# Two cross attentions: the score product from split rows placed by transfers, in the 32-bit rounded type, instead of a full 32-bit product over masked keys

## The reference, cut to what matters

```python
qh, kh, vh = (proj(q, Wq, bq), proj(k, Wk, bk), proj(v, Wv, bv))      # (b, 16, 512 or 77, 8)
scores = einsum('bhqd,bhkd->bhqk', qh, kh) / sqrt(8)
attn = softmax(scores, axis=-1)     # block 3: with a mask, and one more column of zero score in the sum
x = x + proj_out(einsum('bhqk,bhkd->bhqd', attn, vh))
```

## Time and profile before

| | |
|---|---|
| median of 3 runs | 1113.5 us (1104.1 to 1117.23) |
| the profiled execution, its own time | 1112.59 us |
| its span, first to last instruction | 1110.7 us |
| mean granted clock of TensorE | 0.871 |
| busy: PE, VectorE, ScalarE, POOL | 886.1, 599.1, 399.6, 225.2 us |
| l1x, 297 to 462 us | 165 us |
| l3x, 616 to 757 us | 141 us |

### The profile page before, as it was taken

The page is one execution under the profiler, slowest core; times in us unless marked ns, Lnnn a source line. Parts: engine busy times, 40 slices in busy tenths (PEclk is TensorE's granted clock), DMA queues, the critical chain, the costliest instruction groups (busy, mean ns, idle before and its releaser), DMA issues.

```text
span 1110.7 us, 15554 instructions
## 1 busy us (share of the span) xinstructions
PE 886.1 (80%) x5734; PEld 497.6 (45%) x5734; DVE 599.1 (54%) x1614; ACT 399.6 (36%) x687; POOL 225.2 (20%) x228
## 2 busy tenths in 40 slices
PE   5788985986776777569589799976888889886987
PEld 2334553653432343347457434333334334332887
DVE  4455554433535544435473355548687887773553
ACT  2344322332231322111042143331676565555423
POOL 1100051225142122124431000021000100004254
PEclk7799786999985876669889899996999998997999
DMA  9900001132043500031200200021212121103443
GB/s 282 303 25 1 1 31 45 55 94 69 24 128 83 167 25 23 29 90 37 64 2 4 76 1 1 1 61 54 80 54 79 39 74 42 39 20 122 153 156 114
DMA packets 56369, 76.35 MB, mean 69 GB/s; under 512 B 8318, under 2 KB 35070, under 8 KB 55608
## 3 DMA queue, kind: packets, MB, share of 16 engines
q1 hardware_dynamic: 50984, 66.08, 19.1%
q0 software_dynamic: 5312, 9.29, 2.6%
HBM read 46.76 MB, written 31.65 MB: 71 GB/s over the span
## 4 chain that ended last, share of the span: by engine, by line
PE 55%; DVE 20%; issue 10%; ACT 4%; DMA 3%; POOL 3%; another core or an unknown queue 3%; SPq 2%; POOLq 0%; DVEq 0%; ACTq 0%
PE PS L183 48%; DVE KB L1998 5%; PE PS L666 2%; DVE KB L1600 2%; DVE Ht L1514 1%; DVE st L1501 1%; POOL RB L2297 1%; SPq L2359 1%; DVE ON L1667 1%; POOL dbuf L2217 1%; DVE OT L1642 1%; POOL ve L2190 1%; PE PS L674 1%; DVE CX L1642 1%
## 5 line engine op out<-in xcount | busy, mean ns | idle before, releaser
L1998 DVE TENSOR_REDUCE KB<-PS 128x2 fp32r<-128x1024 f32 x128 | 154.4, 1220 | 36.6 <-PE PS L183 35.1
L1277 ACT ACTIVATE PT<-PS 77x512 f32<-77x512 f32 x192 | 98.1, 590 | 178.5 <-PE PS L183 178.5
L183 PE MATMUL PS<-CX 32*77 32x512 f32 (+2 forms) x896 | 129.3, 589 | 22.5 <-DVE OT L1642 10.5
L2190 POOL TENSOR_TENSOR ve<-ve,nh 128x4 f32<-128x4 f32 x40 | 41.3, 1032 | 441.4 <-DVE ve L1509 441.2
L1600 DVE TENSOR_REDUCE KB<-PS 128x16 fp32r<-128x1232 f32 x48 | 69.1, 1439 | 73.8 <-PE PS L183 73.8
L1433 ACT ACTIVATE PT<-PS 128x1024 f32<-128x1024 f32 x74 | 75.6, 1023 | 54.9 <-PE PS L183 52.7
L183 PE MATMUL PS<-QB,KB 64*128 64x512 f32 x256 | 61.9, 480 | 31.1 <-DVE KB L1998 19.7
L183 PEld LDWEIGHTS PS<-CX 32*128 32x128 f32 (+1 forms) x896 | 50.2, 199 | 67.2 <-issue 19.2
L183 PE MATMUL PS<-KB,QB 64*128 64x512 f32 x256 | 66.9, 523 | 6.0 <-DVE KB L1998 4.7
L183 PE MATMUL PS<-PT,VB 77*32 77x512 f32 x384 | 57.3, 672 | 6.7 <-DVE KB L1600 5.0
L183 PE MATMUL PS<-PT,RB 128*32 128x256 f32 x592 | 59.5, 410 | 1.5 <-ACT PT L1433 1.4
(11 more groups left out here) (330 smaller groups left out, 1548.6 us busy)
## 6 DMA issues: line engine op xcount, KB each, us to landing
S<-RA SPq DMA_DIRECT2D x20, 256.0 KB
QB<-zq SPq DMA_DIRECT2D x16, 256.0 KB, 2.7
KB<-zk SPq DMA_DIRECT2D x64, 64.0 KB, 2.4
dbuf<-in_c_fill SPq DMA_DIRECT2D x1, 2580.0 KB, 21.6
RB<-d SPq DMA_DIRECT2D x10, 256.0 KB
o<-CX SPq DMA_DIRECT2D x10, 256.0 KB, 2.3
CX<-RA SPq DMA_DIRECT2D x10, 256.0 KB
RA<-in_l_w SPq DMA_DIRECT2D x1, 2304.0 KB, 11.1
```

Source lines behind the costliest of these rows:

```text
L183: return e.matmul(o, l, r, start=first, stop=last, skip_group_check=True)
L1277: e.activation(slot[s][0:NK, :], PS[0:NK, 4 + j, :], ACT.Exp, bias=0.0, scale=a.scale).then_inc(*expd(i, r, j))
L1998: e.tensor_reduce(o, PS[:, k:k + 2, :], AX, ALU.max).then_inc(*rmax("s", s, t, p2))
L2190: e.tensor_tensor(ve[:, 8 * par + 4:8 * par + 8], ve[:, 8 * par:8 * par + 4], nh[:, :], ALU.pow).then_inc(*rstd(*key))
```

## The change

For l1x and l3x, the score product of `cross_back` alone is replaced. Queries and keys are each split into a rounded part (hi) and a remainder (lo), and laid out so that the 24 rows of one head are (hi, lo, hi) for queries and (hi, hi, lo) for keys; their product is hi*hi + lo*hi + hi*lo. Per unit, POOL makes the two parts (`CAST STG<-CX`, `TENSOR_TENSOR STG<-CX,STG`, each 128x512), SP writes them by three transfers to the DRAM tensor `zq1`, and reads them back by four into `QP1` (`RR<-zq`), a tile of type fp32r at RA's address. Once for l1x and once for l3x the same is done with the keys (128x312). The maximum is still computed from `a.km` and still subtracted by the selector product. As QP1 and KP1 lie over RA, they can be written only after the last expert product of block 0, and the loads of block 3's expert weights move from hook "l1x0" to `first(s)`, 16 pieces of 256 KB in the self attention.

```diff
+        QP1 = [RR[:, 2048 * n:2048 * n + 2048] for n in range(2)]
+        KP1 = RR[:, 6912:8192]
+        QHL = [STG[:, 0:512], STG[:, 512:1024]]
+        KHL = [KN[:, 0:CK], KN[:, 512:512 + CK]]
...
                 for r in range(4):
+                    if not a.expo:
+                        w.wait_ge(*kr1.at("k", a.n0, 3))
+                        w.wait_ge(*ld["l1"].all())
+                        w.wait_ge(*qr1[i % 2].at(i, 3))
                     for j in range(4):
                         w.wait_ge(*banks.take_at(4 + j, expd, i, r, j))
-                        mm(e, PS[0:NK, 4 + j, :], a.km[32 * j:32 * j + 32, b, r, :], Q[32 * j:32 * j + 32, r * a.nq // 4, :], True, False)
+                        if a.expo:
+                            mm(e, PS[0:NK, 4 + j, :], a.km[32 * j:32 * j + 32, b, r, :], Q[32 * j:32 * j + 32, r * a.nq // 4, :], True, False)
+                        else:
+                            mm(e, PS[0:NK, 4 + j, :], KP1[32 * j:32 * j + 24, CK * r + NKP * b:CK * r + NKP * b + NK],
+                               QP1[i % 2][32 * j:32 * j + 24, 512 * r:512 * r + 512], True, False)
...
+            def ahead(i):                                   # gpsimd
...
+                w.wait_ge(*qact.at(i, 0))
+                w.wait_ge(*(qw1[(i - 1) % 2].at(i - 1 if i != 20 else 11, 2) if i > 8 else (None, 0)))
+                e.tensor_copy(QHL[0], Q).then_inc(*split("qhi", i))
+                w.wait_ge(*split.at("qhi", i))
+                e.tensor_tensor(QHL[1], Q, QHL[0].bitcast(F32), ALU.subtract).then_inc(*split("qlo", i))
...
+            def queries(i):                                 # sync
+                w.wait_ge(*qw1[i % 2].at(i, 2))
+                w.wait_ge(*(scored.at(before[i], 3, 3) if before[i] >= 8 else e0.at("d", 2 * NT0 - 1)))
+                w.wait_ge(*down0.at(7))
+                for j in range(4):
+                    e.dma_start(QP1[i % 2][32 * j:32 * j + 24, :].rearrange("p (r c) -> p r c", r=4).bitcast(F32),
+                                zq1[i % 2][4 * j:4 * j + 4, :, :].rearrange("r p c -> p r c")).then_inc(*qr1[i % 2](i, j))
+
+            def ahead(i):                                   # sync
...
+                w.wait_ge(*split.at("qhi", i))
+                e.dma_start(z[:, 0:8, :], QHL[0].bitcast(F32)).then_inc(*qw1[i % 2](i, 0))
+                e.dma_start(z[:, 16:24, :], QHL[0].bitcast(F32)).then_inc(*qw1[i % 2](i, 1))
+                w.wait_ge(*split.at("qlo", i))
+                e.dma_start(z[:, 8:16, :], QHL[1].bitcast(F32)).then_inc(*qw1[i % 2](i, 2))
...
+                w.wait_ge(*scored.at(23, 3, 3))             # sync, first(s)
+                if s < 8:
+                    load("l3f", w1g[:, s, :], A["l3_w1"][s])
+                else:
+                    load("l3f", w2g[:, s - 8, :, :], A["l3_w2"][s - 8].rearrange("(c p) n -> p c n", p=128))
...
                     load("l1f", w2e, A["l1_w2"].rearrange("e (c p) n -> p e c n", p=128))
-                    for b in range(NB):
-                        w.wait_ge(*down0.at(4 + b))
-                    load("l3f", w1g, A["l3_w1"].rearrange("e p n -> p e n"))
-                    load("l3f", w2g, A["l3_w2"].rearrange("e (c p) n -> p e c n", p=128))
```

More of the change, by code:

```diff
@@ L241, in program @@
         zqk = [[nc.dram_tensor(f"z{n}{b}", (512, 512), F32, kind="Internal").ap() for b in range(NB)] for n in "qk"]
+        zq1 = [nc.dram_tensor(f"zq1{n}", (16, 24, 512), F32, kind="Internal").ap() for n in range(2)]
+        zk1 = [nc.dram_tensor(f"zk1{n}", (16, 25, CK), F32, kind="Internal").ap() for n in range(2)]
         x1 = nc.dram_tensor("x1", (NB * S, 128), F32, kind="Internal").ap()
@@ L429, in program @@
         d0e, comb = signal("d0e"), signal("comb")
+        split = signal("split")
         pinit, rstd, xrow = signal("pinit"), signal("rstd"), signal("xrow")
@@ L1173, in prepare @@
                         w.wait_ge(*kcD.at(a.n0 - 1, 0))
+                    if a.n0 == 2:
+                        w.wait_ge(*split.at("klo", 1))
                     if a.expo:
@@ L2204, in norm, with prepare @@
                     add_row(Xb[b], rows[kind], (i,))
+            def ahead(i):
+                kind, b = units[i]
+                yield
+                yield
+                if att[kind].expo:
+                    return
+                Q = queries_at(i)[:, 0, :]
+                w.wait_ge(*qact.at(i, 0))
[3 more added lines that the diff above has]
+                e.tensor_tensor(QHL[1], Q, QHL[0].bitcast(F32), ALU.subtract).then_inc(*split("qlo", i))
+            def prepare(a):
+                if a.expo:
+                    return
+                yield
+                yield
+                w.wait_ge(*kact.at(a.n0, 0))
+                w.wait_ge(*(kw1.at("k", 1, 2) if a.n0 == 2 else (None, 0)))
+                e.tensor_copy(KHL[0], CX[:, 9120:9120 + CK]).then_inc(*split("khi", a.n0))
+                w.wait_ge(*split.at("khi", a.n0))
+                e.tensor_tensor(KHL[1], CX[:, 9120:9120 + CK], KHL[0].bitcast(F32), ALU.subtract).then_inc(*split("klo", a.n0))
+                yield
             def route(b):
@@ L2312, in gpsimd @@
             e.memset(prev[:, 0:8], 0.0).then_inc(*pinit("prev"))
-            order(norm, nothing, nothing, nothing, nothing, nothing, route, capacity, nothing, self_norms, nothing, nothing, nothing, nothing, nothing, tail4,
+            order(norm, ahead, nothing, nothing, nothing, prepare, route, capacity, nothing, self_norms, nothing, nothing, nothing, nothing, nothing, tail4,
                   route3, place3, experts3, nothing, nothing, place0, nothing, gather0, hook)
@@ L2332, in front, with keys @@
                     yield
+                elif kind != "l0x":
+                    if i > 8:
+                        queries(i)
+                    yield
+            def queries(i):
[6 more added lines that the diff above has]
+            def ahead(i):
+                yield
+                yield
+                if units[i][0] == "l0x":
+                    return
+                z = zq1[i % 2]
+                w.wait_ge(*(qr1[i % 2].at(before[i], 3) if before[i] >= 8 else (None, 0)))
+                w.wait_ge(*split.at("qhi", i))
[3 more added lines that the diff above has]
+                e.dma_start(z[:, 8:16, :], QHL[1].bitcast(F32)).then_inc(*qw1[i % 2](i, 2))
+            def keys(n):
+                z = zk1[n - 1]
+                w.wait_ge(*split.at("khi", n))
+                e.dma_start(z[:, 0:8, :], KHL[0].bitcast(F32)).then_inc(*kw1("k", n, 0))
+                e.dma_start(z[:, 8:16, :], KHL[0].bitcast(F32)).then_inc(*kw1("k", n, 1))
+                w.wait_ge(*split.at("klo", n))
+                e.dma_start(z[:, 16:24, :], KHL[1].bitcast(F32)).then_inc(*kw1("k", n, 2))
+                w.wait_ge(*kw1.at("k", n, 2))
+                w.wait_ge(*(scored.at(11, 3, 3) if n == 2 else ld["l1"].all()))
+                for j in range(4):
+                    e.dma_start(KP1[32 * j:32 * j + 25, 0:4 * CK].rearrange("p (r c) -> p r c", r=4).bitcast(F32),
+                                z[4 * j:4 * j + 4, :, :].rearrange("r p c -> p r c")).then_inc(*kr1("k", n, j))
             def self_norms(b):
@@ L2464, in hook @@
                     load("l2w", S2[:, :], A["l2_w"])
+                elif name == "l1k":
+                    keys(1)
+                elif name == "l1q":
+                    queries(8)
                 elif name == "l1x0":
@@ L2490, in hook @@
                     load("l2m", mkf[0:NK, :], A["mfT"])
+                    keys(2)
                 elif name == "l3x1":
@@ L2533, in sync @@
                     load("zero3", z[:, a:a + n], z0[:, 0:n])
+            for z in zk1:
+                load("l1", z[:, 24:25, :], A["c_z"][1][:, 0:1, 0:CK])
             load("zero", dbuf.rearrange("(p t) d -> p (t d)", p=128), A["c_fill"])
-            order(nothing, nothing, front, nothing, nothing, nothing, route, capacity, nothing, self_norms, first, nothing, maxima, nothing, nothing,
+            order(nothing, ahead, front, nothing, nothing, nothing, route, capacity, nothing, self_norms, first, nothing, maxima, nothing, nothing,
                   nothing, nothing, nothing, experts3, nothing, nothing, nothing, experts0, nothing, hook)
```

13 lines of the change are left out of this document (11 added, 2 removed).

## The result

| | before | changed |
|---|---|---|
| median | 1115.37 us (4 runs, 1104.1 to 1117.68) | 1128.76 us (4 runs, 1123.73 to 1132.82) |
| ratio to before | 1 | 1.0133, 95% interval 1.0094 to 1.0172 |
| mean granted clock, profiled run | 0.871 | 0.834 |
| span, profiled run | 1110.7 us | 1124.5 us |

A second measurement on another chip gave 1.0186 (1.0138 to 1.0234). The forecast was 1100 us, its range ended at 1114; the measured time lies above it, where rival E stood. A ratio uses the executions within 1.5% of the fastest of their kernel; that leaves out 5 of 10 for the second run of f32 on the rows with unit 8 on the old path, 4 of 12 for the short product with the memsets on POOL and none for all but the product, so a loss that comes in some executions only is understated.

A forecast was written before the change was run, and what follows sets the result against it. PE was taken to set the pace in most of l3x and part of l1x. Gains 9.1 + 7.25 less 0.5, 1, 0.5 and 2 gave 12.4 us off 1112.6: 1100 us, range 1090 to 1114.

The forecast's parts named there:

- rival E: l3x: with less work on PE its granted clock falls, 3.1 us more for a group; 1125 us, chance 0.09.
- The price of the new product: Score product of a group: 0.65 us saved at the higher clock level, 1.35 us at the lower.
- 5 passes against 2: Score and selector records of a strip: f32 makes two passes, fp32r one, 0.25 us each; 0.76 us saved at most.
- 9.1 us: Saving in l3x: 13 of 16 groups count, 12 at 0.65 us and one at 1.3 us.
- Is there anything that ends later?: Check in one group: VectorE's reduction lets PE come 0.7 us earlier, so the saving of 0.65 us just fits.
- With the clock at 1.00: l3x: its window was to be 8 to 10 us shorter while the granted clock stayed at the full level.
- 7.25 us: Saving in l1x after its first five groups, where the chain is on PE: 0.5 + 4.05 + 2.7.
- 2 us taken here: Whole kernel: allowance for a clock that may fall a little since PE does less.
- If that cover is gone, up to 5 us are to be paid; I take 0.5: Start of l1x: unit 8's first score comes 4.3 to 5.3 us late, mostly hidden by 5.25 us of PE idle time.
- rival C: Start of l1x: unit 8's late first score isn't covered and costs 5 us; 1105 us, chance 0.07.
- POOL and SP: About 17 us of new POOL work costs 1 us, plus 0.5 for slower VectorE; SP's moved loads cost 0.
- Rival D: POOL's splits and VectorE block each other at a shared port, 15 us paid; 1113.5 us, chance 0.09.

The follow-up runs named there:

- f32 on the rows with unit 8 on the old path: Changed kernel with the score product reading the new rows as f32, and unit 8 scored the old way without its wait: ratio 1.0111, then 1.0101.
- short product with the memsets on POOL: Kernel before with an fp32r score product of constants, real scores left out, and the V4 memsets moved to POOL: ratio 0.995.
- all but the product: Changed kernel with splits, transfers, moved loads and waits (not unit 8's), but the old f32 score product of 32 rows: ratio 0.9928.
- both mends: Changed kernel with unit 8 on the old score path without its wait, and the V4 memsets moved from VectorE to POOL: ratios 0.998 and 0.9973.
- short product alone: Kernel before with an fp32r score product of constants in l1x and l3x, real scores left out; no split, transfer or wait added: ratio 1.009.
- memsets moved: Changed kernel with the four memsets of tile V4 moved from VectorE to POOL: ratio 1.0121.
- issued twice: Changed kernel with each new score product issued two times in a row, the second overwriting the first: ratio 1.016, inconclusive.
- splits alone: Kernel before with only POOL's casts and subtractions of queries and keys added; no transfers, new product or new waits on PE: ratio 0.9972.
- unit 8 old: Changed kernel with unit 8 taking its scores from the masked keys and CX, without waiting for the new rows: ratio 1.0134, too wide to tell.

## Why the prediction was wrong, step by step

**The price of the new product: right.** 0.65 was taken, 0.63 measured, by the reading of 5 passes against 2.

**"9.1 us" in l3x: the count was too high.** With the clock held and the memsets away, product and mend gave 7.7 to 8.0 up to 731.23, of which some 6.4 are the product's. In the whole of l3x they gave 4.0 to 6.4, of which 2.7 to 5.1 are the product's: near its end the clock stood at 1.2 GHz for 14 to 17 us (725.6 to 742.7 in the second profile of both mends) where before has 3.4. The step that failed is "Is there anything that ends later?": the 0.7 us of margin was read at one group and used for all. Most groups saved 0.45 to 0.64 us, but at two kinds of place nothing came of it. Where a norm's transposes stand between scores and values, the maximum products stand 6.51 us apart in before (649.55 and 656.06) and 6.52 in the changed kernel (654.22 and 660.74), these rows being the changed kernel's:

```profile
654.22 0.80 PE L183 MATMUL PS<-CX 32*128 32x308 f32 x8 [0.81 <-DVE OT L1666]
...
658.30 0.63 PE L590 MATMUL PS<-ident,Ht 128*128 128x128 f32 x4 [1.04 <-DVE Ht L1538]
...
660.74 0.80 PE L183 MATMUL PS<-CX 32*128 32x308 f32 x8 [0.81 <-DVE OT L1666]
```

The same transposes waited 0.40 us before. The whole saving went into that wait. At the memsets it went into the wait of 1.52.

**"With the clock at 1.00" in l3x, rival E at 0.09: E was the case.** E had the mechanism (less work at the same pace, then the lower level) but looked for it in PE's mean busy share, 90% to 88%, which names no place. The clock fell behind one gap, and that gap stood in the chain of waits as 664.85, memset. E's price was close. From one mask product of the maxima to the next (us):

| | at the memsets | next | with a norm | end of a unit |
|---|---|---|---|---|
| before | 6.45 | 6.85 | 7.88 | 8.73 |
| changed, from 667.95 | 7.07 | 10.10 | 10.95 | 12.87 |
| both mends, 2nd profile | 4.91 | 6.22 | 7.88 | 8.28 |

At the lower level the last three groups took 3.9, 3.1 and 4.6 us more than with the level kept, where E had 3.1. That sum divided the busy time of the window by 16 groups, and 13 stand in it; by 13 it is 4.0. With the clock's fall l3x was 1.5 and 8.5 us longer than before up to 731.23 where it might have been 6.4 shorter.

**"7.25 us" in l1x, and "2 us taken here" for the clock: the largest miss.** From 338.11 to 405.03 l1x became 12.1 us longer, and 3.5 shorter behind that: 8.6 us lost where 7.25 were to be gained. The old product stood at a mean clock of 0.72, a mix of levels, and I let it stand; the step that failed is to take 1.35 a group from a stage whose clock was free to fall. With the short product it is 0.61 alone, and 0.50 to 0.65 in seven profiles with the new data path. The short product alone gained nothing: l1x in the whole was 2.1 and 1.5 us longer in its two profiles, which is no more than the old product showed (1.2 shorter to 2.4 longer in six further profiles). So shown is that the gain isn't there, not that this product alone loses. The loss of 8.6 came with the new rows: 8.6 to 9.5 in four profiles, but 2.9, 3.0 and 5.2 in three more (both mends the first time, memsets moved, issued twice), and 7.1 to 8.6 in three with f32 on these rows. Why is open.

**"If that cover is gone, up to 5 us are to be paid; I take 0.5" (rival C): C was the case too.** The wait was 7.45 us where 4.3 to 5.3 were forecast: from the issue of the first read (312.18) to the score were 6.67 us, against 1.8 + 2.7. Eight reads were issued in a row, unit 9's behind unit 8's, which the sum had left out; that they slowed each other is argued, not tried. The start of l1x was 6 to 8.5 us longer than in the second profile of before, and taking the wait away gave 1.4% beside the memsets' mend. The clock went down in this gap (1.00 until 313, 0.50 from 315); before reached the lower level some us later without it (319 and 328 in its two profiles), so how much of the price is the clock's isn't shown.

**POOL and SP: right.** 612 and 1269 ns, TENSOR_SCALAR at 344 ns; splits alone 0.997. Rival D, whose rule was an exclusive port, didn't show: with 18.5 us more of POOL, VectorE was busy for 600.0 us where it had been 599.1. The moved loads cost nothing either.

**What stays open.** Why the f32 product on 24 rows measured 1.010 and 1.011 where that on 32 rows, in the same program otherwise, measured 0.993: 24 rows in the kernel before moved the clock by 0.008 and the time by 0.24% only, and the programs were not measured side by side (before took 1080.91 and 1082.59 us beside the one and 1111.11 beside the other). One difference was not tried: in the masked keys 8 of the 32 rows aren't zero, in the new rows all 24 may be. And why all but the product was 0.7% faster than before, which neither splits, moved loads nor memsets explain by more than 0.4%.

## What to carry to other kernels

Cutting PE's work in a stage where PE runs at the higher level turns into gaps wherever another engine ends within the saving: go through all groups of the stage for that margin, not one, and look at the gaps that grow, the longest first, since here the clock fell behind the longest one in five of five profiles, and once, with that one gone, behind the next. Where such a gap stands for a reason of its own (here memsets of 2.8 us on VectorE, ahead of a reduction that PE needs), move that first. The stage that already stood between the two levels, l1x, gained nothing from less work on PE; and a new path by DRAM for the first unit of a stage has to be ready before PE gets there, or that unit stays on the old path.

## What the runs showed of the hardware

- The granted clock fell ahead of the same instruction in all five profiles of the short product with the memsets on VectorE (changed kernel twice, short product alone, unit 8 old, issued twice): behind waits of 1.30 to 1.53 us for the reduction and of 0.81 us, the maximum product took 1.41 us in each. It stayed at 1.2 GHz for 20 to 34 us although PE was busy nearly all of that time (30.00 of 30.00 us in the changed kernel). In before, waits of 0.88 and 0.81 at the place left it at 2.4 GHz; with the f32 product over 24 rows the same two waits were followed by 1.2 GHz in three of three profiles.
- A kernel with less work on PE and nothing added was slower by 0.9%: 1.009 for the short product alone, 0.995 once the gap was mended (each beside before on its own chip).
- An fp32r score product of 24 rows and a selector product over four strips take 0.63 us at 2.4 GHz, where two f32 records and a selector record took 1.26.
